# Transposing in the tile loop of a routed expert network: by DMA into SBUF instead of by TensorE into PSUM

## What is computed

```python
# x: (4, 1024, 1024) f32, so T = 4096 tokens of H = 1024
x = x + xattn(layernorm(x), ctx)          # fp8-like quantised 1024x1024 product per batch
h = layernorm(x).reshape(T, 1024)
scores = sigmoid(h @ gate_w)              # 32 experts, 4 groups, 2 groups masked, top 6
weights, selected = ...                   # weights normalised over the 6
g = ragged_dot(h[sorted], w_gate); u = ragged_dot(h[sorted], w_up)      # 1024 -> 704
d = ragged_dot(silu(g) * u, w_down)                                     # 704 -> 1024
shared = silu(h @ sw_gate) * (h @ sw_up) @ sw_down                      # 1024 -> 1408 -> 1024
out = x + sum_k(weights_k * d_k) + shared
```

## Time and profile before

| what | value |
|---|---|
| time, median of 3 runs | 7532.23 us (7532.09 to 7548.77) |
| profiled execution, span from the first to the last instruction | 7518.3 us |
| instructions | 118517 |
| PE busy | 6885.7 us (92%) |
| PE weight loads (beside the matmuls) | 4126.7 us (55%) |
| DVE busy | 1906.1 us (25%) |
| ACT busy | 1500.9 us (20%) |
| POOL busy | 3376.3 us (45%) |
| moved by DMA | 949.13 MB, mean 126 GB/s |

### The profile page before, as it was taken

How to read it: one execution, slowest core, us unless ns; L and a number is a source line. 1 busy time by engine, 2 the same in 40 slices (tenths; PEclk the granted TensorE clock), 3 DMA queues, 4 the chain that set the end, 5 groups by cost and what they waited for, 6 DMA issues and landing times.

```text
span 7518.3 us, 118517 instructions
## 1 busy us (share of the span) xinstructions
PE 6885.7 (92%) x46550; PEld 4126.7 (55%) x46551; DVE 1906.1 (25%) x3125; ACT 1500.9 (20%) x1750; POOL 3376.3 (45%) x2190
## 2 busy tenths in 40 slices
PE   1455559999999999999999999999999999999999
PEld 0233335666666666666565655556666666655655
DVE  3555582111111111111111111111111111114555
ACT  1333331111111111111111111111111111111111
POOL 3555574460455433455334553455356346433222
PEclk9777779999999999999999999999999999999999
DMA  1222236971233322233222332333233223326555
GB/s 50 79 84 88 82 117 265 380 298 52 94 109 104 109 92 92 98 107 119 92 93 102 106 117 92 104 104 112 96 107 124 96 92 122 110 74 230 227 225 205
DMA packets 313376, 949.13 MB, mean 126 GB/s; under 512 B 38272, under 2 KB 38272, under 8 KB 313344
## 3 DMA queue, kind: packets, MB, share of 16 engines
q1 hardware_dynamic: 179712, 470.50, 18.5%
q10 hardware_dynamic: 73728, 268.47, 9.9%
q0 software_dynamic: 59904, 209.75, 7.3%
HBM read 647.10 MB, written 309.85 MB: 127 GB/s over the span
## 4 chain that ended last, share of the span: by engine, by line
PE 85%; issue 7%; POOL 4%; DVE 2%; DMA 2%; ACT 0%; SPq 0%; POOLq 0%; DVEq 0%; ACTq 0%
PE ps_gu L618 52%; PE ps_d L618 23%; PE ps_t L609 3%; PE ps_t L719 3%; POOL wts L469 2%; PE ps_d L736 2%; PE ps_d L734 2%; DMA wts<-in_x 1%; POOL wts L474 1%; POOL wts L460 0%; DVE amax_p L1014 0%; DVE stats_q L1072 0%; DVE wts L1244 0%; DVE wts L1260 0%; POOL wts L462 0%
## 5 line engine op out<-in xcount | busy, mean ns | idle before, releaser
L618 PE MATMUL ps_gu<-wts,xT 128*128 128x352 f16 x26112 | 3944.6, 313 | 11.2 <-issue 9.9
L618 PEld LDWEIGHTS ps_gu<-wts,xT 128*128 128x128 f16 x26112 | 2541.0, 98 | 1331.3 <-issue 11.7
L444 POOL TENSOR_SCALAR wts<-stage 128x1408 f16<-128x1408 f32 (+1 forms) x476 | 587.9, 1235 | 2719.2 <-PE ps_d L736 2700.6
L618 PE MATMUL ps_d<-wts,hT 128*128 128x512 f16 x8160 | 1805.7, 379 | 1.0 <-DVE hT L1216 1.0
L618 PEld LDWEIGHTS ps_d<-wts,hT 128*128 128x128 f16 x8160 | 785.7, 98 | 901.2 <-ACT hT L937 1.2
L447 POOL TENSOR_TENSOR wts<-stage,wts 128x1408 f16<-128x1408 f32 (+1 forms) x476 | 1260.2, 2647 | 39.7
L1204 DVE SCALAR_TENSOR_TENSOR hid<-ps_gu,sil 128x704 f32<-128x704 f32 x272 | 242.3, 891 | 3654.9 <-ACT sil L928 3654.9
L928 ACT ACTIVATE sil<-ps_gu 128x704 f32<-128x704 f32 x272 | 205.9, 757 | 3458.5 <-PE ps_gu L618 3458.5
L445 POOL TENSOR_SCALAR stage<-stage 128x1408 f32<-128x1408 f32 (+1 forms) x476 | 592.6, 1245 | 0.0
L942 ACT ACTIVATE dout<-ps_d 128x1024 f32<-128x1024 f32 x240 | 245.7, 1024 | 1399.3 <-PE ps_d L736 1399.3
L1216 DVE COPY hT<-ps_t 128x640 f16<-128x640 f16 x272 | 133.2, 490 | 1193.0 <-PE ps_t L719 1193.0
(11 more groups left out here) (152 smaller groups left out, 3440.9 us busy)
## 6 DMA issues: line engine op xcount, KB each, us to landing
xin<-rows_x ACTq DMA_DIRECT2D x272, 512.0 KB
rows_d<-dout ACTq DMA_DIRECT2D x240, 512.0 KB, 2.7
stage<-in_L_ffn_w_down SPq DMA_DIRECT2D x384, 256.0 KB, 2.9
stage<-in_L_ffn_w_gate SPq DMA_DIRECT2D x256, 352.0 KB, 3.1
stage<-in_L_ffn_w_up SPq DMA_DIRECT2D x256, 352.0 KB, 3.6
wts<-in_x SPq DMA_DIRECT2D x64, 512.0 KB, 5.6
rows_x<-wts SPq DMA_DIRECT2D x64, 512.0 KB, 3.1
wts<-rows_x SPq DMA_DIRECT2D x64, 512.0 KB, 6.5
```

Source lines behind the costliest of these rows:

```text
L444: g.tensor_scalar(high, raw, WSCALE, 1.0, ALU.mult, ALU.mult).then_inc(conv_step, 1)
L618: ins = nc.tensor.matmul(dst[c], left, right[c], start=(first and a == 0), stop=(last and a == 2))
```

## The change

The transposes of `xin` and of `hid_hl` leave PE. ACT issues a transposing DMA for each instead: `turn_x(n)` reads the 128 x 2048 values of `xin` and writes `xT`; `turn_h(n)` reads the 128 x 1408 values of `hid_hl` and writes `hT`, which now has 11 blocks of 128 columns. `take_xt` and `take_ht` on ACT and DVE are gone, `ps_t` is no longer used in the loop. The semaphores trx, xt_high and xt_low become one, `xt_in`, which the DMA raises by 16; trh, ht_high and ht_low become `ht_in`.

ACT's order around tile n becomes: wait for gate_up(n), turn_x(n+1), silu(n), high_of_hidden(n) (which waits for the h transpose before, since it overwrites `hid_hl`), wait for the x transpose to land (`xin_free`), load_x(n+2), turn_h(n) (which waits for the low half and for down(n-1)), store_d(n-1). PE's becomes gate_up(n), down(n-1). Tile 0's x transpose waits for the last logits product, which reads `xT`.

```diff
@@ tensor
-            def tr_x(n):
-                pe.wait_ge(xin_in, n * 16 + 16)
-                transposes(xin).then_inc(trx, 1)
...
-            def tr_h(n):
-                pe.wait_ge(hid_high, n + 1)
-                pe.wait_ge(hid_low, n + 1)
-
-                for a, blocks in ((0, KM), (1, KM - 1)):
-                    for k in range(blocks):
-                        at = a * KM * P + k * P
-                        last = nc.tensor.transpose(ps_t[:, a, k * P:(k + 1) * P], hid_hl[:, at:at + P], ident[:, :])
-                last.then_inc(trh, 1)
...
-            def tile(n, entry=None, first=False, last=False):
+            def tile(n, entry=None, first=False):
                 ready, buf, buf_before = entry_of(n) if entry is None else entry
 
                 pe.wait_ge(weights_ready, ready)
-                pe.wait_ge(xt_high, n + 1)
-                pe.wait_ge(xt_low, n + 1)
+                pe.wait_ge(xt_in, n * 16 + 16)
                 if not first:
                     pe.wait_ge(hid_done, n)
                 by_buffer(gate_up, n, buf)
                 if not first:
-                    pe.wait_ge(ht_high, n)
-                    pe.wait_ge(ht_low, n)
-                if not last:
-                    tr_x(n + 1)
-                if not first:
+                    pe.wait_ge(ht_in, n * 16)
                     pe.wait_ge(d_free, n)
                     by_buffer(down, n - 1, buf_before)
-                if not last:
-                    pe.wait_ge(xt_high, n + 2)
-                    pe.wait_ge(xt_low, n + 2)
-                tr_h(n)
@@ scalar
-            def take_xt(n):
-                act.wait_ge(trx, n + 1)
-                a.activation(xT[:, 0, :, :], ps_t[:, 0, :].rearrange("p (k n) -> p k n", k=KH), ACT.Copy)\
-                    .then_inc(xt_high, 1)
+            def turn_x(n):
+                act.wait_ge(xin_in, n * 16 + 16)
+                act.sem_inc(act_turn, 1)
+                act.dma_start_transpose(xT[:, :, :, :].rearrange("p a k n -> p (a k) n"),
+                                        xin[:, :, :].rearrange("p a d -> p (a d)")).then_inc(xt_in, 16)
+
+            def xin_free(n):
+                act.wait_ge(xt_in, n * 16 + 16)
...
-            def high_of_hidden(n):
+            def high_of_hidden(n, first=False):
                 act.wait_ge(hid_done, n + 1)
+                if not first:
+                    act.wait_ge(ht_in, n * 16)
...
-            def take_ht(n):
-                act.wait_ge(trh, n + 1)
-                a.activation(hT[:, 0, 0:KM * P], ps_t[:, 0, 0:KM * P], ACT.Copy).then_inc(ht_high, 1)
+            def turn_h(n, first=False):
+                act.wait_ge(hid_high, n + 1)
+                act.wait_ge(hid_low, n + 1)
+                if not first:
+                    act.wait_ge(down_done, n)
+                act.sem_inc(act_turn, 1)
+                act.dma_start_transpose(hT[:, :, :], hid_hl[:, :]).then_inc(ht_in, 16)
...
-            def tile(n, next_row=None, last=False, store=False):
-
+            def tile(n, next_row=None, first=False, last=False, store=False):
+
+                act.wait_ge(gu_done, n + 1)
+                if not last:
+                    turn_x(n + 1)
                 silu(n)
-                if not last:
-                    take_xt(n + 1)
+                high_of_hidden(n, first)
                 if next_row is not None:
+                    xin_free(n + 1)
                     load_x(n + 2, next_row)
-                high_of_hidden(n)
+                turn_h(n, first)
                 if store:
                     store_d(n - 1)
-                take_ht(n)
```

More of the change, by code:

```diff
@@ L232, in build @@
                              "slots_ready", "tables_ready", "pad_out"))
[L234 to L239, removed]
+        xin_in, xt_in, gu_done, silu_done = (sem(n) for n in ("xin_in", "xt_in", "gu_done", "silu_done"))
+        hid_done, hid_high, hid_low, ht_in, down_done, d_free, d_out = (sem(n) for n in (
+            "hid_done", "hid_high", "hid_low", "ht_in", "down_done", "d_free", "d_out"))
+        act_turn, dve_turn, pool_turn = (sem(n) for n in ("act_turn", "dve_turn", "pool_turn"))
         comb_step, comb_done, o_out = (sem(n) for n in ("comb_step", "comb_done", "o_out"))
@@ L729, in down @@
                 for k in range(KM - 1):
-                    three(outs, hT[:, 0, k * P:(k + 1) * P], hT[:, 1, k * P:(k + 1) * P], weights(0, k),
-                          weights(1, k), k == 0, False)
+                    three(outs, hT[:, k, :], hT[:, KM + k, :], weights(0, k), weights(1, k), k == 0, False)
                 for c in range(2):
-                    nc.tensor.matmul(outs[c], hT[:, 0, K_LAST:KM * P], weights(0, KM - 1)[c], start=False, stop=False)
+                    nc.tensor.matmul(outs[c], hT[:, KM - 1, :], weights(0, KM - 1)[c], start=False, stop=False)
                 for c in range(2):
-                    ins = nc.tensor.matmul(outs[c], hT[0:M_LAST, 0, K_LAST:KM * P], weights(1, KM - 1, M_LAST)[c],
+                    ins = nc.tensor.matmul(outs[c], hT[0:M_LAST, KM - 1, :], weights(1, KM - 1, M_LAST)[c],
                                            start=False, stop=True)
@@ L800, in _ @@
                 tile(n_tiles + i, (E + 2, 1, 1))
-            tile(n_tiles + (TT - 1), (E + 2, 1, 1), last=True)
+            tile(n_tiles + (TT - 1), (E + 2, 1, 1))
             drain_tile(n_tiles + (TT - 1), 1)
@@ L944, in store_d @@
                 act.dma_start(rows_d[ds(n * P, P), :], dout[:, :]).then_inc(d_out, 16)
-            def tile(n, next_row=None, last=False, store=False):
+            def tile(n, next_row=None, first=False, last=False, store=False):
+                act.wait_ge(gu_done, n + 1)
+                if not last:
+                    turn_x(n + 1)
                 silu(n)
-                if not last:
-                    take_xt(n + 1)
+                high_of_hidden(n, first)
                 if next_row is not None:
+                    xin_free(n + 1)
                     load_x(n + 2, next_row)
-                high_of_hidden(n)
+                turn_h(n, first)
                 if store:
                     store_d(n - 1)
-                take_ht(n)
             act.wait_ge(x2_out, 16 * TT + 16)
             load_x(0, 0)
-            take_xt(0)
+            act.wait_ge(logits_done, TT)
+            turn_x(0)
+            xin_free(0)
             load_x(1, P)
-            tile(0, 2 * P)
+            tile(0, 2 * P, first=True)
             with act.Fori(1, A_LAST) as n:
@@ L1212, in low_of_hidden, with tile @@
                                 ALU.subtract).then_inc(hid_low, 1)
-            def take_ht(n):
-                dve.wait_ge(trh, n + 1)
-                v.tensor_copy(hT[:, 1, 0:K_LAST], ps_t[:, 1, 0:K_LAST]).then_inc(ht_low, 1)
-            def tile(n, last=False, before=None):
+            def tile(n, before=None):
                 hidden(n)
-                if not last:
-                    take_xt(n + 1)
                 low_of_hidden(n)
@@ L1225, in tile @@
                     take_down(*before)
-                take_ht(n)
-                if before is not None:
                     combine(*before)
@@ L1349, in _ @@
                 tile(n_tiles + (q * 2 + 2), before=(q * 2 + 1, 1, q))
-            tile(n_tiles + (TT - 1), last=True, before=(TT - 2, 0, TT // 2 - 1))
+            tile(n_tiles + (TT - 1), before=(TT - 2, 0, TT // 2 - 1))
             take_down(TT - 1, 1, TT // 2 - 1)
```

12 lines of the change are left out of this document (2 added, 10 removed).

## The result

The changed kernel takes 7732.0 us, the median of four runs (7723.9 to 7739.8), against 7534.0 for the kernel before, the median of four: a ratio of 1.0246, with an interval of 1.0231 to 1.026. It is 2.5% slower where 4.4% faster was forecast; the sign was wrong, and the time lies in the range because the range took in rival A.

The account below looks back on a forecast made before the run. TensorE (PE), busy 92%, was taken to bound the kernel; span 7518.3 - 413 (transposes gone) + 78 (scatter tiles) + 1 (ends) = 7184 us, with 13.9 around the span 7198 us, 4.4% faster. Range 7100 to 9300 us.

Parts of the forecast that it names:

- rival A: In front of gate_up(n+1), x's transpose lands late, from 8.6 us changing the sign; 7540 to 9300 us, chance 0.31.
- the landing of x under load: x's DMA transpose before the next gate_up: 11 us while rows are scattered, 5 to 7 in the final pass.
- the quiet landing: x's DMA transpose in the expert stage: 5 us, between 2.7 and 6.5, free up to 7.1 behind down.
- rivals B: x's transpose worked as 16 blocks one after the other: period 40.0 us, 12050 us in all, chance 0.09.
- D: The transposing DMA works as an element-wise copy, many times slower than block by block; chance 0.05.
- The weights stay covered: Weight loads before an expert: POOL's shortest wait falls from 68.53 to about 59 us, still covered.
- the loaded stage: Tiles while rows are scattered: x lands 3.9 us over its cover, 20 tiles, 78 us lost (bounds 44 and 118).
- h is free there: h's DMA transpose while rows are scattered: covered by gate_up's 14.33 us, about twice the store's 7.0; cost nothing.
- the final pass: Last 32 tiles: x lands in 5 to 7 us, nothing lost; at 10.0 it would be 93 us.
- no clock lost: PE's 3.9 us pauses in the tiles with scattered rows: no clock loss, as after an earlier 2.88 us pause.
- the issue: x's transpose issue on ACT's queue before silu: 0.35 us plain, 5.6 for 16, free up to 5.7; cost nothing.
- the ends: Tile 0 saves 2.2 us more, the open last h transpose loses 3.2; together +1 us.

Follow-up runs that it names:

- the third experiment: Against the changed kernel, only the h transpose by DMA, in all tiles, with x kept on TensorE: 7433.3 us, ratio 0.9874 to the kernel before.
- the first experiment: Against the changed kernel, DMA transposes only from tile 30 to the last expert tile, TensorE's elsewhere: 7238.0 us, ratio 0.9616 to the kernel before.
- the mix: Against the changed kernel, x by DMA in the expert tiles only, h by DMA there and in the final pass: 7243.4 us, ratio 0.9596 to the kernel before.

## Why the prediction was wrong

The step that failed is the landing of x under load: 11 us were put down beside the scatter and 5 to 7 in the final pass, and 27.7 and 11.4 were measured. The mechanism of the quiet tile was right.

**Right.** PE sets the pace and its transposes are links of the chain; 1.52 us a tile go; the quiet landing was put at 5 us, between the rows of 2.7 and 6.5, and is 3.8 to the last packet, 4.3 alone by the profile's measure; that 5 was near is of no weight, since anything up to 7.1 gives the same time. It is hidden behind down's 7.1, and the quiet tile is 21.87 where 21.9 was forecast: rivals B (block by block) and D fall with it. The weights stay covered: POOL's shortest wait for PE was to be about 59 us and is 59.74.

```profile
4834.90 1.36 POOL L443 TENSOR_SCALAR wts<-stage 128x1408 f16<-128x1408 f32 x1 [59.74 <-PE ps_d L720]
```

The last down started 3.8 us after the one before it had ended (7695.03 + 0.60 to 7699.45), where about 5 was forecast. In the quiet stage, the pause behind it included, 23 us were missed, as good as all of it the 28 late tiles, of which the one that ends at 3034.47 above is an example.

**Wrong: the loaded stage, 278 us.** The step was to add 4.3 us to a 5 us transpose, or multiply it by 2.6, because a plain store of the same size goes from 2.7 to 7.0 there. A transpose is not slowed like a plain transfer: 3.8 became 27.7, a factor of 7, and the same is shown by itself (4.3 to 25.9, beside a plain 3.2 to 8.5). The forecast for tiles 0 to 22 was 44.6 us over before (78 - 22 x 1.52), and 322.4 was measured. The bounds of 9.3 and 13 had no room for it, since both ends came from the same plain row. The kernel before had a steeper one: its weight loads of 352 KB, first in the quiet stage, then from 1123 to 1620 us, lost a factor of 4 where the store of dout lost 2.6.

```profile
stage<-in_L_ffn_w_gate SPq DMA_DIRECT2D x236, 352.0 KB, 3.1
...
stage<-in_L_ffn_w_gate SPq DMA_DIRECT2D x4, 352.0 KB, 12.6
```

By that factor a 5 us transpose would be put at 20, over the 8.6 that turns the sign of those tiles; it is an estimate, and still short of 27.7. Rival A had the mechanism, its place and its point of decision at 8.6 us. Its price for the loaded tiles (at about 18, between 14.3 and 26) was nearer, and its 10.0 comes near the 11.4 of the final pass; its claim on the quiet tiles was wrong.

**Wrong: h is free there.** It was covered up to 14.33 us, and "twice the 7.0" seemed enough. 19.3 is over it, and PE stood 87.6 us for it. In the tile above this wait of 6.72 us costs nothing by itself, because x lands later still. What h costs alone is in the third experiment: 25.7 us a tile beside the scatter instead of 22.8. Both transposes go through ACT's queue, and from 1414 to 1787 us the first packet of x came 1.0 to 1.1 us behind the last of h, nine times running. That held x back little: its first packet came 3.4 to 5.1 us behind its issue there, and 3.5 to 4.0 where h was long through, in the changed kernel with silu first.

**Wrong: the final pass, 235 us.** With 5 to 7 us nothing was to be lost; the row of 10.0 for rows_d was named and priced at 93 us as a bound. 11.4 is the median there, and PE stood in front of most gate_ups, up to 20.9 us. Two in a row:

```profile
7109.31 16.06 PE L617 MATMUL ps_gu<-wts,xT 128*128 128x352 f16 x96 [4.42 <-DMA xT<-xin]
...
7138.51 16.81 PE L617 MATMUL ps_gu<-wts,xT 128*128 128x352 f16 x96 [5.70 <-DMA xT<-xin]
```

Here too the row next to it, POOL's gathers, was in the profile, and the kernel with all by DMA from tile 30 on puts the whole loss of this stage on x; with x alone by DMA it is 28.5 a tile too.

**Wrong: no clock lost.** The two pauses of the earlier trace rows were read for the first, 2.88 with no cost, not for the second, 9.88 with 2.5 us. The pauses that came were longer than the first. Of the gate_ups of after from tile 1 on, the 38 behind a pause of 4 to 22 us took 15.8 to 18.2 us instead of 14.48; the down above took 8.82 instead of 6.64. All matmuls together: 106 us. Where the waits are gone, as in the first experiment, the clock is 0.98 to 1.00 again.

**Wrong in size, no harm by itself: the issue.** 0.35 each for a plain one, up to 5.6 for 16 was the bound. It is 2.0 us for x when quiet and 13.5 in the scatter stage, so silu at 1538.40 starts 14.4 us behind the end of gate_up. It was still not the end of the chain: with silu first the scatter stage is the same 39.2 a tile. The bound of 5.7 us held in the quiet stage and was passed in the others.

**A view read too coarsely.** PE was not busy in every microsecond from 1123 us on: the earlier trace rows has 372.18 of 377 in the first stage, which changes nothing in the sum. The DMA share of 0.84 in the same row is a mean over 377 us. Two shorter stretches of the kernel before show what is in it:

```profile
1123.00:1220.00 97.00, 92.18 (x622) 56.69 (x623) 45.40 (x54) 18.12 (x21) 40.00 (x45) 0.95 0.39 142
1220.00:1500.00 280.00, 280.00 (x1883) 168.21 (x1881) 35.28 (x60) 51.02 (x60) 135.95 (x159) 1.00 0.99 380
```

Once the scatter runs the DMA engines are full, 0.99 at 380 GB/s. That left little room for 3456 more packets a tile (2048 for x and 1408 for h).

The terms add up: 278 + 235 + 23 + 2 for the ends is 538, the distance from the forecast span of 7184 to 7722.3.

**Why x lands in 28 us with h by DMA too, and mostly in 5.5 to 8.9 without.** In the packet records of the two pairs of kernels (x alone and both, each with silu in its two places), the x transposes that were issued from 1230 us to the last scatter packet are sorted here by how many packets of POOL's queue started between their own first and last packet. With fewer than 150 they landed in 7.5 us at the median (29 of them, 4.0 to 11.1); with over 600, in 28.5 (26 of them, 23.5 to 40.6); eight lie between. In the kernels without the h transpose a tile is short enough for the x transposes to fall between POOL's batches nearly always; with h, a tile of 47 us holds two batches 23.5 us apart, and a landing of 28 can't miss one. A long landing also meets more packets, so the count alone proves nothing; the lone transpose with indirect stores added beside it shows which is the cause. That the phase holds itself is argued, not shown.

The Trainium skill, page "Advanced Engine Details and Errata", section "X-Bar Transpose (TRN2)", says that a transposing DMA is as fast as a regular one. The runs come near this when it has the DMA engines to itself (4.3 us against 3.2) and differ beside SP's loads (14.5 against 7.0) and beside POOL's indirect stores (25.9 against 8.5). The Trainium skill, page "VectorE: DVE Perf Modes", section "The three transpose paths", has 1309 ns for one block by DMA; this doesn't add up over blocks, since 16 of them landed in 3.8 us. By either page the answer would have been the same in all 272 tiles, and it was not.

## What to carry to other kernels

A single-buffered transfer that must land between two matmul groups is worth what its landing is in each stage of the loop, so take the stage with the most traffic of other queues, over its own window, and don't carry a slowdown from a plain transfer to a transposing one. Where one stage has room and another hasn't, choose the path per stage: the mix is 4.0% faster than before, the same change everywhere 2.5% slower. Put the compute that others wait for in front of a transposing DMA's issue on the same queue; two swapped lines were worth 335 us (by the ratios 355) where PE needed the result at once.

## What the runs showed of the hardware

- A transposing DMA runs in packets of 256 bytes, 2048 for 512 KB. Counted off in sixteens by their start, the sixteens follow each other 0.019 us apart at the median when quiet. In the scatter stage about half of those of x and 0.7 of those of h come over 0.1 us behind the one before, at the median of these 0.18 us. An estimate from this: 128 sixteens, each 0.17 behind the one before, would be 21.8 us, most of the 27.7. That each waits for a 4096-byte packet of another queue (0.159 us at the median) fits this stage and is not shown; beside SP's 4096-byte loads the same would give over 20 us, and 14.5 was measured.
- The issue of such a DMA holds the issuing engine: 2.0 us at the median for 512 KB and 1.4 for 352 KB when quiet, 13.5 and up to 24 us for 512 KB in the scatter stage, against 0.35 for a plain one.
- It slows the others too. The last scatter packet came at 1622 us before, at 1893 after, and at 1666 with x alone; the rate from 1123 to 1500 us fell from 319 to 244 GB/s with the DMA engines busier than before.
- Pauses of 4 to 22 us were followed by gate_ups of 15.8 to 18.2 us instead of 14.5, and the granted clock in the slowest 200 us was 0.76 on the mean. Behind the pause of 14.91 us at 1507.84 it was at 1.2 GHz until 1511.3 and then at 2.4.
